# Two hops of a graph attention kernel: one operand of VectorE's large products in PSUM, and zero partitions under TensorE's short operands

## What is computed

```python
def _agg(ent, rel, head, tail, etype, fc_w, fc_b):
    a_input = jnp.concatenate([ent[head], ent[tail]], axis=-1)
    e = jax.nn.leaky_relu(jnp.sum((a_input @ fc_w.T + fc_b) * rel[etype], axis=-1), negative_slope=0.2)
    m = jax.ops.segment_max(e, head, num_segments=n)
    exp_e = jnp.exp(e - m[head])
    alpha = exp_e / jax.ops.segment_sum(exp_e, head, num_segments=n)[head]
    return jax.ops.segment_sum(ent[tail] * alpha[:, None], head, num_segments=n) + ent

for _ in range(2):
    ent = _agg(ent, relation_emb, head, tail, edge_type, fc_w, fc_b)
    ent = ent / jnp.maximum(jnp.linalg.norm(ent, axis=-1, keepdims=True), 1e-12)
out = layernorm(x + ent)
```

## Time and profile before

| | us |
|---|---|
| median of 3 runs | 2908.32 |
| their range | 2891.43 to 2922.03 |
| the profiled execution | 2870.03 |
| its span, first to last instruction | 2867.7 |
| DVE busy in the span | 1848.4 (64%) |
| POOL busy | 1805.7 (63%) |
| PE busy | 1218.3 (42%) |
| ACT busy | 866.2 (30%) |

### The profile page before, as it was taken

The page is one execution under the profiler, slowest core; times in us unless marked ns, Lnnn a source line. Parts: engine busy times, 40 slices in busy tenths (PEclk is TensorE's granted clock), DMA queues, the critical chain, the costliest instruction groups (busy, mean ns, idle before and its releaser), DMA issues. The chain is left out here.

```text
span 2867.7 us, 22941 instructions
## 1 busy us (share of the span) xinstructions
PE 1218.3 (42%) x4597; PEld 818.2 (29%) x4597; DVE 1848.4 (64%) x3677; ACT 866.2 (30%) x1585; POOL 1805.7 (63%) x1607
## 2 busy tenths in 40 slices
PE   4688801354423544245433534444344345343300
PEld 4577701122211222123212423232223223222200
DVE  6867864286562865546655559877667667766753
ACT  2232304375453754445631212111111111111111
POOL 1000047377774777757777238877777787777776
PEclk9555555555555555555555556665655555566555
DMA  2333333254432444335433133222222222222210
GB/s 68 89 109 103 104 70 84 52 147 131 126 91 71 130 132 131 86 95 150 122 87 114 51 112 89 82 85 79 61 83 87 72 66 84 86 58 66 60 44 13
DMA packets 91815, 255.95 MB, mean 89 GB/s; under 512 B 31782, under 2 KB 39047, under 8 KB 91771
## 3 DMA queue, kind: packets, MB, share of 16 engines
q1 hardware_dynamic: 41403, 183.66, 20.8%
q0 software_dynamic: 50368, 71.78, 11.4%
HBM read 157.76 MB, written 102.23 MB: 91 GB/s over the span
## 5 line engine op out<-in xcount | busy, mean ns | idle before, releaser
L572 POOL DMA_INDIRECT area<-rows,gi x1176 | 1330.2, 1131 | 487.4 <-issue 367.7
L620 POOL DMA_INDIRECT out<-area,place x392 | 459.3, 1172 | 119.5 <-issue 119.5
L765 PE MATMUL psR<-area,row_t 128*98 128x512 f16 (+1 forms) x896 | 302.7, 504 | 454.3 <-DVE area L1191 335.9
L748 PE MATMUL psR<-area 128*128 128x392 f16 x392 | 198.5, 506 | 445.2 <-issue 406.3
L670 PE MATMUL psP<-V,vT 65*125 65x40 f32 (+1 forms) x1586 | 323.4, 393 | 86.1 <-issue 56.6
L670 PEld LDWEIGHTS psP<-V,vT 65*125 65x125 f32 (+1 forms) x1586 | 316.0, 310 | 104.7 <-issue 62.4
L765 PEld LDWEIGHTS psR<-area,row_t 128*98 128x98 f16 x896 | 141.5, 173 | 610.4 <-DVE area L1191 351.9
L908 ACT ACTIVATE area<-area 128x896 f32<-128x896 f32 x84 | 79.8, 950 | 586.2 <-DVE area L1270 433.6
L872 ACT ACTIVATE area<-iota_h,half_hi 128x392 f16<-128x392 f16 x392 | 238.9, 609 | 16.8 <-issue 15.4
L1269 DVE TENSOR_TENSOR area<-SM,rd 128x896 f32<-128x896 f32 x56 | 93.6, 1671 | 206.6 <-DMA out<-area,place 205.4
L774 PE MATMUL psT<-ones,area 98*128 98x1 f32 x700 | 152.6, 352 | 173.5 <-DVE area L1191 131.1
(11 more groups left out here) (269 smaller groups left out, 2296.4 us busy)
## 6 DMA issues: line engine op xcount, KB each, us to landing
rows<-area SPq DMA_DIRECT2D x50, 787.5 KB
area<-tail_digits SPq DMA_DIRECT2D x28, 896.0 KB
rows<-area SPq DMA_DIRECT2D x28, 735.0 KB
area<-rows SPq DMA_DIRECT2D x28, 735.0 KB
area<-rows SPq DMA_DIRECT2D x25, 787.5 KB
area<-rows,gi POOLq DMA_INDIRECT x1176
head_xs<-area SPq DMA_DIRECT2D x28, 448.0 KB
area<-head_xs SPq DMA_DIRECT2D x28, 448.0 KB
```

The source lines that it names most:

```text
L572: pool.indirect_dma_start(out=to[:, b, k, 0:tab.shape[1]], out_offset=None, in_=tab, in_offset=bass.IndirectOffsetOnAxis(ap=gi[:, b, n, k: ...
L620: pool.indirect_dma_start(out=out, out_offset=bass.IndirectOffsetOnAxis(ap=place[:, b, k:k + 1].bitcast(U32), axis=0), in_=rowO[:, b, k, 0 ...
L748: te.matmul(psC, sign_lo[:, (s0 + k) % KS, :], sign_hi[:, (s0 + k) % KS, :], start=static and t0 + k == 0, stop=True, skip_group_check=True)
L765: te.matmul(psR[g % 2][0:HH, 0:w], row_t[:, n, c, :], hot_lo[:, c, 4 * g * P:4 * g * P + w], start=c == 0 and n == 0, stop=c == HB - 1 and ...
```

## The change

Small factors and some of the large intermediate results that DVE used to read from SBUF are placed in parts of PSUM banks that TensorE does not use in that stretch, so that a large two-input instruction of DVE has at most one of its inputs in SBUF.

- In hop 2 that holds for all of them: the type mask, the head scores, `ex`, `decay`, `first_end`, `rd`, `rs`, `mean`, and the first result of each pair of products of the finish (`via`) lie in `psT` and `psP` ("held").
- In the 24 loop chunks of hop 1 copies of `iota_r`, `first_end`, `rd`, `rs`, `m`, `r` and `t` lie in `psR[1]` ("kept"). `ex`, `decay`, the type mask and `vv` stay in SBUF, so L1333, L1346, L1359, L1361, L1270 and L1304 still read both inputs from SBUF. Two small instructions a chunk are new, which write `kept_m` and `kept_r`.
- `vT` and `V` get 128 partitions in place of 65, with zeros in the new ones; DVE clears `vT`'s at the very start. The row sums of L774 take all 128 partitions of `chosen` in place of 98; the rest is cleared once.

The core of the diff ("..." where lines are left out):

```diff
-        V = sb("V", [CO, 2 * R])
+        V = sb("V", [P, 2 * R])
-        vT = sb("vT", [CO, KN * P])
+        vT = sb("vT", [P, KN * P])
+        flatT = psT[:, :, :].rearrange("p n x -> p (n x)")
+        held = flatT[:, 0:K * C].rearrange("p (k c) -> p k c", c=C)
+        held_A = flatT[:, 0:K * R].rearrange("p (k r) -> p k r", r=R)
+        held_typ = flatT[:, K * R:2 * K * R].rearrange("p (k r) -> p k r", r=R)
...
+        kept_end, keep = psR[1][:, 0:T], psR[1][:, T:]
+        kept_rd, kept_rs, kept_iota = keep[:, 0:K], keep[:, K:2 * K], keep[:, 2 * K:2 * K + R]
...
+        held_ex = psP[:, 1, 512 - 2 * K:512].rearrange("p (n k) -> p n k", n=2)
+        held_decay = psP[:, :, :].rearrange("p n x -> p (n x)")[:, 0:CO * (K + 1)].rearrange("p (c k) -> p c k", k=K + 1)
...
+            pool.wait_ge(s_zero, 1)
             gp.memset(vT[C:CO, :], 1.0).then_inc(s_set, 1)
-            gp.memset(V[C:CO, :], 0.0).then_inc(s_set, 1)
+            pool.wait_ge(s_set, 7)
+            gp.memset(V[C:P, :], 0.0).then_inc(s_set, 1)
...
-                    te.matmul(sums[:, k:k + 1], chosen[0:HH, k * P:(k + 1) * P], ones[0:HH, 0:1], start=True, stop=True)
+                    te.matmul(sums[:, k:k + 1], chosen[:, k * P:(k + 1) * P], ones[:, 0:1], start=True, stop=True)
...
+                    ex_, decay_ = (ex[:, :, :], decay) if h == 0 else (held_ex, held_decay)
...
+            ve.memset(vT[C:P, :], 0.0).then_inc(s_zero, 1)
...
+                if kept:
+                    link(ve.tensor_scalar(kept_m, m, 1.0, None, ALU.mult))
+                ve.scalar_tensor_tensor(xc[0:PN, b, :, :], wide(kept_m if kept else m, KN, C, PN), 1.0 / C, X,
+                                        ALU.mult, ALU.subtract).then_inc(s_cen, 1)
...
+                if kept:
+                    link(ve.tensor_scalar(kept_r, r, 1.0, None, ALU.mult))
+                link(ve.tensor_tensor(xr[0:PN, b, :, 0:WT], xr[0:PN, b, :, 0:WT], wide(kept_r if kept else r, KN, WT, PN), ALU.mult))
...
+                t_ = kept_t if kept else t
+                link(ve.scalar_tensor_tensor(t_, s, -1.0, dev, ALU.mult, ALU.mult))
+                ve.tensor_tensor(xc[0:PN, b, :, :], xc[0:PN, b, :, :], wide(t_, KN, C, PN), ALU.mult).then_inc(s_node, 1)
...
+                if isinstance(j, int) and j == 0:
+                    link(ve.memset(chosen[96:P, :], 0.0))
...
+                via, rd_, rs_, mean_ = (vv, kept_rd if kept else rd, kept_rs if kept else rs, mean) if h == 0 else (held[:, 0:K0, :], held_rd, held_rs, held_mean)
+                link(ve.tensor_tensor(via, agg, wide(rd_[:, 0:K0], K0), ALU.mult))
+                ve.tensor_tensor(vv, via, rowsH[:, :, 0:C], ALU.add).then_inc(s_sq, 1)
...
-                    link(ve.tensor_tensor(vv, vv, wide(rs[:, 0:K0], K0), ALU.mult))
-                    link(ve.tensor_tensor(vv, vv, rowsX, ALU.add))
+                    link(ve.tensor_tensor(via, vv, wide(rs_[:, 0:K0], K0), ALU.mult))
+                    link(ve.tensor_tensor(vv, via, rowsX, ALU.add))
...
+                    typ_, iota_ = (typ, kept_iota if kept else iota_r) if h == 0 else (held_typ, held_iota)
+                    ex_, decay_, rd_, part_ = (ex, decay, kept_rd if kept else rd, part) if h == 0 else (held_ex, held_decay, held_rd, held_part)
...
-                        fa, la = (cap[:, n * R:(n + 1) * R, :].rearrange("p r k -> p k r") for n in range(2))
-                        last_A = last_row[:, A0:A0 + R]
+                        fa, la = held_A, cap[:, 0:R, :].rearrange("p r k -> p k r")
...
-                        fe = first_end[:, cc]
+                        fe = ((kept_end if kept else first_end) if h == 0 else held_end)[:, cc]
...
+                link(ve.tensor_copy(held_iota, iota_r[:, :]))
+                link(ve.tensor_copy(held_end, first_end[:, :]))
+                link(ve.memset(held_decay[:, :, 0], 0.0))
```

More of the change, by code:

```diff
@@ L253, in build_gnn @@
         psK, psY = psR
+        flatT = psT[:, :, :].rearrange("p n x -> p (n x)")
+        held = flatT[:, 0:K * C].rearrange("p (k c) -> p k c", c=C)
+        held_A = flatT[:, 0:K * R].rearrange("p (k r) -> p k r", r=R)
+        held_typ = flatT[:, K * R:2 * K * R].rearrange("p (k r) -> p k r", r=R)
+        held_part = flatT[:, 1024 - CO - 1:1024]
+        small = flatT[:, 1024:1536]
+        held_end, small = small[:, 0:T], small[:, T:]
+        held_rd, held_rs, held_mean, held_iota, held_first, held_last = (
+            small[:, a:a + n] for a, n in ((0, K), (K, K), (2 * K, K), (3 * K, R), (3 * K + R, R), (3 * K + 2 * R, R)))
+        kept_end, keep = psR[1][:, 0:T], psR[1][:, T:]
+        kept_rd, kept_rs, kept_iota = keep[:, 0:K], keep[:, K:2 * K], keep[:, 2 * K:2 * K + R]
+        kept_m, kept_r, kept_t = (keep[0:PN, 2 * K + R + n * KN:2 * K + R + (n + 1) * KN] for n in range(3))
+        assert T + 2 * K + R + 3 * KN <= 512
+        held_ex = psP[:, 1, 512 - 2 * K:512].rearrange("p (n k) -> p n k", n=2)
+        held_decay = psP[:, :, :].rearrange("p n x -> p (n x)")[:, 0:CO * (K + 1)].rearrange("p (c k) -> p c k", k=K + 1)
+        assert K * C <= 1024 - CO - 1 and 3 * K + 3 * R + T <= 512 and CO * (K + 1) <= 1024 - 2 * K
         s_src = sem("heads_loaded")
@@ L1277, in finish @@
                         dve.wait_ge(s_dump[b], 16 * i)
-                    ve.tensor_tensor(rowO[:, b, 0:K0, 0:C], vv, wide(rs[:, 0:K0], K0), ALU.mult).then_inc(s_v, 1)
+                    ve.tensor_tensor(rowO[:, b, 0:K0, 0:C], vv, wide(rs_[:, 0:K0], K0), ALU.mult).then_inc(s_v, 1)
                     meanwhile[1]()
@@ L1320, in _, with chunk @@
                 link(ve.memset(first[:, :], 0.0))
-                def chunk(j, b, static, ahead, i, nodes=h == 0, look=None, taking=None, h=h, nr=nr, r0=r0, e0=e0, x0=x0):
+                def chunk(j, b, static, ahead, i, nodes=h == 0, look=None, taking=None, kept=False, h=h, nr=nr, r0=r0, e0=e0, x0=x0):
                     cc = cols(j)
@@ L1395, in chunk @@
                     finish(h, K, b, H, rowX[:, b, :, :], r0 + j * nr, j + 1, S[:, 0:C, 1:K + 1].rearrange("p c k -> p k c"), (capture, rest), free,
-                           static and i == 0, i)
+                           static and i == 0, i, kept)
                     if h == 1:
@@ L1406, in pair @@
                         chunk(i * 2 + b, b, static, True, i, look=(q, 1 - b, i + 1 + b) if h == 1 else None,
-                              taking=(q - 1,) if h == 1 and not (static and b == 0) else None)
+                              taking=(q - 1,) if h == 1 and not (static and b == 0) else None,
+                              kept=h == 0)
                 link.base += link.n
@@ L1444, in _ @@
                 link(ve.tensor_scalar(first[:, C:CO], first[:, C:CO], 1e-30, None, ALU.max))
-                link(ve.reciprocal(rd[:, 0:1], first[:, C:CO]))
+                link(ve.reciprocal((rd if h == 0 else held_rd)[:, 0:1], first[:, C:CO]))
                 dve.wait_ge(s_sg, 16 + 32 * h)
```

64 lines of the change are left out of this document (31 added, 33 removed).

## The result

| | time, us | runs | ratio to before, 95% interval |
|---|---|---|---|
| kernel before, first record | 2912.2 | 4 | |
| changed kernel, first record | 3311.0 (3297.1 to 3314.3) | 4 | 1.147, 1.137 to 1.157 |
| kernel before, chip 4 | 2768.3 | 9 | |
| changed kernel, chip 4 (`f1_changed`) | 2551.2 | 2 | 0.9215, 0.918 to 0.925 |

The forecast was 2699 us, 209 less than before. On the first record the changed kernel took 399 us more than the kernel before; on chip 4 it took 217 us less. The two chips run the same program, and the difference between them can be read in TensorE's rows. The record doesn't name the first chip, so I call it that.

A forecast was written before the change was run, and what follows sets the result against it. POOL's queue of indirect DMAs was taken to bound both hops. On the profiled execution 2870.0 - 154 (hop 2) - 58 (hop 1) + 3 = 2661 us; the same -209 us on the median 2908.3 gave 2699 us, range 2640 to 2760.

The forecast's parts named there:

- The queue, its lateness and where it goes: Both hops: POOL's indirect DMAs set the pace, some late behind DVE's two-SBUF-input instructions; PSUM inputs save 154 and 58 us.
- The sum: Whole kernel: 154 us from hop 2 and 58 from hop 1, less 3 us of added work, make 209 us saved.
- the two terms: The forecast savings in the hops: 154 us in hop 2 and 58 us in hop 1.
- PSUM costs DVE nothing: DVE's instructions in both hops: a PSUM operand adds zero time, read from products of 564 and 567 ns.
- both rivals on DVE's side: Hop 2: slower PSUM instructions make DVE the bound, 2766 us (chance 0.05), or slower than before, 3074 us (chance 0.02).
- The padding does nothing to the clock and nothing in the sort: TensorE: padded products leave the granted clock and the sort's 59.6 us of DVE waits unchanged, taken as zero.
- In the hops no long wait is for TensorE: Both hops: no engine waits long for TensorE, so padding and TensorE's work there were given no time.
- 119.7 us of POOL's waits for indices: Hop 1: POOL's waits for DVE's indices, 119.7 us at six places, were left unchanged in the sum.
- the list: Four rivals: clock rises 2669 us (0.10), DVE bounds hop 2 2766 (0.05), slower 3074 (0.02), no effect 2908 (0.05).
- The one on the slower side: Hop 2: PSUM instructions slow DVE so strongly that the kernel is slower than before, 3074 us; chance 0.02.

The follow-up runs named there:

- g2: Changed kernel with its PSUM operands in hop 2 alone, hop 1 computing from SBUF as before; chip 8: 2609.3 us, 0.945 of the kernel before.
- g3: Changed kernel with its PSUM operands in hop 1 alone, hop 2 computing from SBUF as before; chip 8: 2708.2 us, 0.980 of the kernel before.
- e2: Kernel before with only the padding to 128 rows added; chip 8: 2763.1 us against 2767.1 of the kernel before (0.999).
- f3: Kernel before with only the padding to 128 rows added; chip 4: 2764.7 us against 2768.3 of the kernel before (1.000).
- e3: Changed kernel with only the row sums back at 98 rows, projections still at 128; chip 8: 2552.8 us against 2767.1 of the kernel before.
- e1: Changed kernel with only its padding taken back (65 and 98 rows); chip 8: 2549.6 us against 2767.1 of the kernel before (0.922).
- f2: Changed kernel without its padding (65 and 98 rows); chip 4: 2552.8 us against 2768.3 of the kernel before.
- g4: Changed kernel with each matmul of the projections and row sums issued twice; chip 8: 2666.6 us against 2762.4 of the kernel before.
- i1: Kernel before with only the padding to 128 rows added; chip 11: 2912.1 us against 2915.7 of the kernel before.
- l1: Changed kernel without its padding (65 and 98 rows); chip 3: 3241.0 us against 2873.7 of the kernel before (1.128).
- m1: Changed kernel with idle drains and memsets added on POOL in both hops to slow them; chip 15: 2906.4 us against 2854.6 of the kernel before.

## Why the prediction was wrong

**The queue, its lateness and where it goes: right.** On chips without standstills each step came out. Hop 2: mean gather 951 ns and write 991 ns (forecast under 980 and 1020); saving 1224 - 1067 = 157 us (forecast 154). Over the medians of before there is 392 x 0.004 + 392 x 0.005 = 3.5 us left (forecast 12). POOL's rows in 1640 to 2540 us of `f1_changed`:

```profile
L641 POOL DMA_INDIRECT out<-area,place x365 | 361.6, 991 | 111.3 <-issue 110.6 <-DVE gi L1174 0.6
L593 POOL DMA_INDIRECT area<-rows,gi x336 | 319.4, 951 | 102.4 <-issue 102.4
```

The period and DVE's wait for writes in it, which were 41.5 and 8.2 us:

```profile
1999.07 1.67 DVE L1301 TENSOR_TENSOR psT<-SM,psT 128x896 f32<-128x896 f32 x1 [2.94 <-DMA out<-area,place]
...
2034.71 1.67 DVE L1301 TENSOR_TENSOR psT<-SM,psT 128x896 f32<-128x896 f32 x1 [2.71 <-DMA out<-area,place]
```

That is 35.6 us and 2.7 to 2.9 us, against 36 and 2.7. Hop 1: mean gather 1036 ns (1.03 us), saving 53 us (58), with late gathers left at L1395 and L1397 (L1359 and L1361 of before) and the new ones at L1302 (L1270), 24 of them, 0.69 us each, against 0.65. The sum was 209 us; `f1_changed` gave 217, and `g2` and `g3` show the two terms apart.

**PSUM costs DVE nothing: right.** The product of 896 columns takes 1.67 us with its output in PSUM, as it did in SBUF, and the scan with `decay` in PSUM 2.19 us, as in the earlier trace rows. With that both rivals on DVE's side fall.

**The padding does nothing to the clock and nothing in the sort: right.** `e2` and `f3` are within 0.3% of before. The sort's wait differs by a few us from trace to trace, with the padding (53.6 us in `f1_changed`, 58.6 in `e3`) as without (53.6 in `e1`, 56.9 in `f2`), and the mean granted clock from 31 to 380 us is 0.59 to 0.61 in all of them.

**"In the hops no long wait is for TensorE": this is the step that failed.** It was read from the waits of DVE and POOL, and it is true of TensorE's work, as `g4` shows. It was false of the trace that I had. In that trace PE waited 406.3 us ahead of L748 for "issue":

```profile
PEld psR L748 <- issue: 507.5, 279, 54.8
PE psR L748 <- issue: 406.3, 292, 54.6
```

With the longest at 54.6 us, this is no row of an engine that issues freely. The kernel before with its padding on chip 4 (`f3`), where L751 is L748, has this instead:

```profile
PE psR L751 <- issue: 38.1, 176, 0.3
```

And the DRAIN of 58.4 us behind projections that take 6.2 us stood in the trace too. I took "issue" for time that costs nothing. So the kernel before was already losing time to its chip (about 145 us against the others), and I carried its standstills over unchanged, in a sum for a kernel whose hops run closer together. I had also put 119.7 us of POOL's waits for indices down as not touched by the change; on chip 4 they are 23.6 us in `f3` and 27 us in the changed kernel (23.4 at L1172, 4.0 at L1174). So most of them came with this chip's standstills, and they are the term that grew to 806 and ate the 209 us. In the terms of the prediction: the queue's busy time fell as forecast, but the waits ahead of it, which the sum left as they were, grew by 686 us.

**The rival that came true was not on the list.** The one on the slower side (3074 us against 3311 measured) had the direction alone, with DVE as the bound, not TensorE. What speaks for the cause as far as it was found: TensorE stands still or crawls for some 20 to 60 us at a time on some chips (the first, 3, 11 and 15; the factor of 13 is read on chip 11 alone) and not on others (0, 1, 4, 5 and 8). The zero rows aren't needed for it: they cost nothing alone (`i1`), and without them the loss stays (`l1`). With a slower pace the long ones were gone from hop 1 (`m1`, on a chip of its own). In hop 2 of the changed kernel on the first chip the chunk is then one chain through TensorE: row sums of 33.2 us with their late drain (2308.85 to 2342.06), 0.8 us to the row products and 9.2 us of these, then 8.6 us for DVE's last picks before the next row sums start at 2360.73, 51.9 us in all, and 51.7 is the usual period there. Each hit makes TensorE late, so that the next work comes bunched, and that may bring on the next hit; this last step is argued, not shown.

**What stays open.** Why the change turns 501 us of late drains into 1393, and why hop 2's row sums are hit in nearly every chunk even at 45.2 us: the pace, the operands in PSUM, the bunching, or for `m1` chip 15 itself. No kernel separated them: none with the operands in PSUM in one hop alone ran on such a chip, none slowed the changed kernel on a chip where it was timed as it is, and the kernel before has a trace on one such chip only. What in the chip slows TensorE isn't seen in any record.

## What to carry to other kernels

Read TensorE's "issue" waits by their longest one and compare each DRAIN with the matmuls in front of it: a drain that ends tens of us after the last recorded matmul is time in which no busy row shows TensorE, and it isn't a constant that a forecast may carry over. A saving of some hundred us in one queue is only as safe as the slack of the engine that has the chip's standstills, so time both kernels on more than one chip before a verdict. Indirect DMAs of GpSimd that end late beside large DVE instructions with two SBUF inputs lose that lateness when one input moves to PSUM (hop 2's mean gather went from 1184 to 951 ns), at no cost to DVE that any row shows.

## What was unexpected of the hardware

- One program, several chips: the kernel before took 2762 to 2768 us on five of them (0, 1, 4, 5, 8), and 2855 to 2916 us on 3, 11, 15 and the first, which may be one of these; the changed one took 2550 to 2554 us on the five (with its zero rows on chip 4, without them on all), 3241 us on chip 3 (without) and 3311 us on the first (with).
- On chip 11 equal f32 records of one line came 2.8 us apart in place of 0.21, at a granted clock of 0.50 in the records throughout, and went back to 0.21 us with no pause in between. This happened in 25 of 28 blocks, 19 to 25 us each.
- Most of the late drains are behind f32 work, not all: the sign rows' f16 products (L769) came through with 0.8 us at most in `l1`, where in the kernel before 39 of them (L748) were 1 to 2.8 us late, but the f16 row products of hop 2 (L786) were up to 16 us late in `l1`, 115 us in all.
- Twice the f32 work brought no such stretch on chip 8 (`g4`).
- A drain and a memset of 0.42 us on GpSimd took 0.77 us together.
